# A four-layer graph network with a mixture of experts: the gates applied in the expert loop, the mean taken from the stored rows, no meeting ahead of the output pass

## The reference

```python
m = segment_sum(h[src], dst) * rsqrt(deg_in)
x = m @ W_gc + b_gc + feats @ W_res + b_res
vals, idx = top_k(x @ Wg + bg, 2)
gates = softmax(vals)                       # two gates a node
h1 = gelu(rows_of_expert @ w1[e] + b1[e])
y_s = h1 @ w2[e] + b2[e]                    # one row for each (node, pick)
core = zeros(N, D).at[tok_s].add(g_s[:, None] * y_s)
y = x + core
mean, var = mean(y, axis=0), mean((y - mean) ** 2, axis=0)
out = (y - mean) * rsqrt(var + 1e-5) * gamma + beta
# and around it: x = layernorm(x + out)
```

## Time and profile before

| | us |
|---|---|
| median of three runs | 2047.52 |
| lowest and highest | 2045.85, 2050.57 |
| span of the profiled execution | 2045.9 |
| TensorE busy in it | 1805.1 (88%) |
| VectorE, ScalarE, GpSimd busy | 887.9, 498.7, 492.5 |
| expert loop, from the first chunk of steady work to the last rows | about 1615 to 1935 |
| from the last expert rows to the output pass | 1935 to 2011 |
| output pass | 2011 to 2046 |

### The profile page before, as it was taken

One profiled execution on the slowest core, in us unless ns is written; L12 is line 12 of the kernel. 1 busy time (PEld: TensorE's weight loads), 2 busy tenths in 40 slices (PEclk: granted clock), 3 DMA queues, 4 the chain that ended last, 5 costly groups with the idle time before them and its releaser, 6 DMA issues. The chain is left out here.

```text
span 2045.9 us, 34276 instructions
## 1 busy us (share of the span) xinstructions
PE 1805.1 (88%) x9529; PEld 1440.3 (70%) x9563; DVE 887.9 (43%) x2701; ACT 498.7 (24%) x1301; POOL 492.5 (24%) x858
## 2 busy tenths in 40 slices
PE   4888885999899989999999999989999699999830
PEld 2455554788688868878878878867777588888720
DVE  7877663444534421122321137756766212222145
ACT  0134444322222311111111111111111132232252
POOL 1021222311111100000000002216666632332244
PEclk7999997999999989999999999989999799999955
DMA  4188999999678858877768888868876699999931
GB/s 129 53 293 299 318 317 354 311 327 319 224 259 269 263 182 290 291 243 241 239 213 289 289 266 290 290 212 260 258 250 199 209 377 374 375 375 375 351 127 63
DMA packets 279214, 545.09 MB, mean 266 GB/s; under 512 B 18214, under 2 KB 201040, under 8 KB 275920
## 3 DMA queue, kind: packets, MB, share of 16 engines
q1 hardware_dynamic: 269280, 525.30, 77.1%
q0 software_dynamic: 8032, 17.60, 2.3%
q10 hardware_dynamic: 1808, 1.08, 0.3%
HBM read 415.19 MB, written 128.72 MB: 266 GB/s over the span
## 5 line engine op out<-in xcount | busy, mean ns | idle before, releaser
L1069 PE MATMUL psum<-xsa,blk 128*128 128x512 f32 x2500 | 642.2, 406 | 17.8 <-DVEq L381 8.2
L1069 PEld LDWEIGHTS psum<-xsa,blk 128*128 128x128 f32 x2500 | 462.9, 191 | 106.9 <-issue 11.1
L1069 PE MATMUL psum<-xsb,blk 128*128 128x512 f32 (+1 forms) x1875 | 415.7, 369 | 5.9 <-DVEq L381 5.9
L1069 PEld LDWEIGHTS psum<-xsb,blk 128*128 128x128 f32 x1875 | 321.8, 190 | 64.6 <-issue 7.2
L1835 POOL TENSOR_SCALAR ve<-mv 128x1 f32<-128x1 f32 x75 | 16.9, 225 | 802.6 <-DVE mv L1546 802.6
L1431 DVE TENSOR_SCALAR onehots<-counts_scratch 128x348 bf16<-128x348 f16 x464 | 161.7, 373 | 87.8 <-issue 47.1
L971 PE MATMUL psum<-onehots 128*128 128x349 bf16 x464 | 149.4, 322 | 40.3 <-DVE onehots L1436 38.2
L563 PE MATMUL psum<-route,expert_weights 128*128 128x128 f32 x1360 | 170.9, 280 | 0.1
L974 PE MATMUL psum<-zrow 128*128 128x512 bf16 x431 | 164.8, 390 | 0.0
L563 PEld LDWEIGHTS psum<-route,expert_weights 128*128 128x128 f32 x1360 | 161.4, 195 | 1.3 <-DVE route L675 0.5
L573 PE MATMUL psum<-expert_weights,route 128*128 128x256 f32 x672 | 159.1, 380 | 0.0
(11 more groups left out here) (309 smaller groups left out, 2077.4 us busy)
## 6 DMA issues: line engine op xcount, KB each, us to landing
blk<-counts_src_on_rows SPq DMA_DIRECT2D x125, 832.0 KB, 5.2
blk<-counts_src_on_rows SPq DMA_DIRECT2D x125, 768.0 KB, 4.8
expert_weights<-in_L_gnn_w SPq DMA_DIRECT2D x176, 512.0 KB, 6.0
blk<-counts_dst_on_rows SPq DMA_DIRECT2D x50, 832.0 KB, 4.5
counts_dst_on_rows<-band_rows SPq DMA_DIRECT2D x25, 1600.0 KB, 8.2
blk<-counts_dst_on_rows SPq DMA_DIRECT2D x50, 768.0 KB, 4.2
counts_src_on_rows<-blk SPq DMA_DIRECT2D x13, 1600.0 KB, 8.7
counts_src_on_rows<-rblk SPq DMA_DIRECT2D x12, 1600.0 KB, 9.8
```

What stands on the lines that cost most here:

```text
L1069: mm = e.matmul(o, blk[n][:, k * P:(k + 1) * P], XS[:, k, :, 0:Fw], start=(k == 0), stop=(k == T - 1 and not own))
```

## The change

Each pick's gate travels with its number. In the last graph pass ScalarE takes one Exp a tile (`gap_exp`, behind `picks_made`) and GpSimd makes the two gates by three one-column operations at the head of its turn (`l3_gates`). `ids` has two columns, pick number and gate; unused rows have gate 0. SP loads both columns, TensorE turns both, and VectorE keeps `pick_of` and `gate_of`. In the expert loop VectorE scales b2 by the gate and makes `yout` = product * gate + scaled b2. It then adds `yout` to V2, so that after the loop V2 + R2 is the sum of y over each partition; R2 is the sum of X4 over the tiles, made ahead of the loop. One product with ones gives the mean, and X4 is centred before the stored rows are back. The stored rows lie now by partition (`ybuf` row p * 50 + 2t + k), and no engine scales them. GpSimd adds nothing any more: TensorE adds all 25 tiles of squares. The `combine` meeting is gone, and several one-time semaphores are joined (`bn_steps`, `ident_set`).

```diff
+            def l3_gates(i, par):
+                e.wait_ge(S("gap_exped"), i + 1)
+                if i:
+                    e.wait_ge(S("gates_made"), 3 * i)
+                e.tensor_scalar(exps[:, 1:2], exps[:, 0:1], 1.0, None, ALU.add).then_inc(S("gates_made"), 1)
+                e.wait_ge(S("gates_made"), 3 * i + 1)
+                e.tensor_tensor(pick[:, i, 0, 1:2], exps[:, 1:2], minus[:, :], ALU.pow).then_inc(S("gates_made"), 1)
+                e.wait_ge(S("gates_made"), 3 * i + 2)
+                e.tensor_tensor(pick[:, i, 1, 1:2], exps[:, 0:1], pick[:, i, 0, 1:2], ALU.mult).then_inc(S("gates_made"), 1)
             def l3_ids(i, par):
+                e.wait_ge(S("gates_made"), 3 * (i + 1))
                 for k in range(TOP):
                     e.indirect_dma_start(out=ids, out_offset=bass.IndirectOffsetOnAxis(ap=slot_to[:, k, i:i + 1], axis=0),
-                                         in_=pick_id[:, k, i:i + 1], in_offset=None).then_inc(S("ids_scattered"), 16)
+                                         in_=pick[:, i, k, :], in_offset=None).then_inc(S("ids_scattered"), 16)
...
-            pipeline(e, [(2, l3_first), (1, l3_keep), (2, l3_scatter), (2, l3_last), (2, l3_ids)], unrolled=True)
+            pipeline(e, [(2, l3_gates), (2, l3_first), (1, l3_keep), (2, l3_scatter), (2, l3_last), (2, l3_ids)], unrolled=True)
...
+            def gap_exp(i, par):
+                e.wait_ge(S("picks_made"), i + 1)
+                if i:
+                    e.wait_ge(S("gates_made"), 3 * i)
+                e.activation(exps[:, 0:1], top_val[:, i, 0:1], ACT.Exp, scale=-1.0, bias=top_val[:, i, 1:2])\
+                    .then_inc(S("gap_exped"), 1)
+            run("l3", [low("l3", F, ndst), (2, gap_exp), (1, copy("l3", "x_turned", "xT", flat(tT2), pT2)),
...
-            e.dma_start(pick_rows[0:NCH, :], ids[0:NCH * P, :].rearrange("(c p) a -> c (p a)", p=P)).then_inc(S("inputs_loaded"), 16)
+            e.dma_start(pick_rows[0:NCH, :, :], ids[0:NCH * P, :].rearrange("(c p) a -> c p a", p=P)).then_inc(S("inputs_loaded"), 16)
...
-                e.dma_start(picked_rows[:, lo:hi, :, :].rearrange("p t k f -> p t (k f)"),
-                            ybuf[TOP * lo * P:TOP * hi * P, :].rearrange("(t p k) f -> p t (k f)", t=hi - lo, p=P))\
+                e.dma_start(picked_rows[:, lo:hi, :, :].rearrange("p t k f -> p (t k f)"),
+                            ybuf[0:TOP * NP, :].rearrange("(p r) f -> p (r f)", p=P)[:, TOP * lo * F:TOP * hi * F])\
                     .then_inc(S(f"outs_in{g}"), 16)
...
-            phase_end(e, "combine")
...
+            for a in range(2):
+                mm = e.transpose(psum[:, 6, a * NCH:(a + 1) * NCH], pick_rows[0:NCH, :, a], identF[0:NCH, 0:NCH])
+            mm.then_inc(S("ids_turned"), 1)
...
+            e.wait_ge(S("node_sums"), 1)
+            e.matmul(psum[:, 0, 0:F], ones[:, :], V2[:, :], start=True, stop=True).then_inc(S("bn_summed"), 1)
+            for g, (lo, hi) in enumerate(COMBINED):
+                e.wait_ge(S("squared"), g + 1)
+                for t in range(lo, hi):
+                    mm = e.matmul(psum[:, 1, 0:F], ones[:, :], picked_rows[:, t, 1, :], start=(t == 0), stop=(t == T - 1))
+            mm.then_inc(S("bn_summed"), 1)
...
-                        e.activation(v, v, ACT.Copy, scale=gate[:, k, t:t + 1]).then_inc(S("picks_scaled"), 1)
...
+            e.wait_ge(S("tile_x4_kept"), past("l3", "x4_kept") + T)
+            st.done(e.tensor_reduce(R2[:, :], X4[:, 0:T - 1, :].rearrange("p t f -> p f t"), AX.X, ALU.add))
+            st.done(e.scalar_tensor_tensor(R2[:, :], X4[:, T - 1, :], valid[:, T - 1:T], R2[:, :], ALU.mult, ALU.add))
+            e.memset(V2[:, :], 0.0).then_inc(S("rows_added"), 1)
             e.wait_ge(S("ids_turned"), 1)
+            e.tensor_copy(pick_of, psum[:, 6, 0:NCH]).then_inc(S("picks_known"), 1)
+            st.done(e.tensor_copy(gate_of, psum[:, 6, NCH:2 * NCH]))
...
+                    e.wait_ge(S(f"b2_in{n}"), 16 * j + 16)
+                    carry_wait(e)
+                    e.tensor_scalar(b2s[n], b2s[n], gate_of[:, bass.ds(c, 1)], None, ALU.mult).then_inc(S("bias_scaled"), 1)
+                    e.wait_ge(S("bias_scaled"), c + 1)
                     e.wait_ge(S("chunk_summed"), c + 1)
-                    e.wait_ge(S(f"b2_in{n}"), 16 * j + 16)
                     e.wait_ge(S(f"rows_stored{n}"), 16 * j)
-                    e.tensor_tensor(yout[n], psum[:, 4 + par, 0:F], b2s[n], ALU.add)\
+                    carry_wait(e)
+                    e.scalar_tensor_tensor(yout[n], psum[:, 4 + par, 0:F], gate_of[:, bass.ds(c, 1)], b2s[n], ALU.mult, ALU.add)\
                         .then_inc(S("chunk_made"), 1)
+                    e.wait_ge(S("rows_added"), c + 1)
+                    e.wait_ge(S("chunk_made"), c + 3)
+                    carry_wait(e)
+                    e.tensor_tensor(V2[:, :], V2[:, :], yout[n], ALU.add).then_inc(S("rows_added"), 1)
...
+            e.tensor_tensor(V2[:, :], V2[:, :], R2[:, :], ALU.add).then_inc(S("node_sums"), 1)
+            e.wait_ge(S("bn_summed"), 1)
+            st.done(e.tensor_scalar(G[:, :], psum[:, 0, 0:F], 1.0 / N, None, ALU.mult))
+            for g, (lo, hi) in enumerate(COMBINED):
+                e.tensor_tensor(X4[:, lo:hi, :], X4[:, lo:hi, :], G[:, :].unsqueeze(1).to_broadcast([P, hi - lo, F]), ALU.subtract)\
+                    .then_inc(S("centred"), 1)
+            e.wait_ge(S("centred"), len(COMBINED))
+            for g, (lo, hi) in enumerate(COMBINED):
+                e.wait_ge(S(f"outs_in{g}"), 16)
...
-                        ins = e.tensor_tensor(added[:, n, :], added[:, n, :], v, ALU.add)
...
-            phase_end(e, "combine")
```

107 lines of the change are left out of this document (29 added, 78 removed).

## The result

The changed kernel takes 2025.8 us (median of four runs, 2024.4 to 2034.3) against 2048.2 us of the kernel before in the same session (2045.9 to 2050.6). The ratio is 0.990 with an interval of 0.9886 to 0.9914. That is a gain of 22 us where 35 were forecast, and the time lies above the range of 2008.5 to 2021. The profiled execution has a span of 2023.2 us, 22.7 less than before.

The account below looks back on a forecast made before the run. TensorE was taken to bound the expert loop, three waits the tail. 2045.9 - 30.6 - 4.9 + 0.05 + 0.6 + 0.25 = 2011.3 us of span, plus 1.6 to the median, rounded to 2013; range 2008.5 to 2021.

Parts of the forecast that it names:

- What bounds the kernel: Whole kernel: TensorE busy 99.87 of 100 us in the loop; behind it gate products, GpSimd's additions and the meeting.
- Parts 1 and 2: Tail and meeting, behind the expert loop: variance read 30.6 us sooner, and 4.9 us less without the meeting.
- The covered centring: Tail: VectorE's added work and centring, 10.1 us plus hand-overs, hidden behind the stored rows' way out and back.
- the rise of the clock: Tail: TensorE's denser squares bring its clock to full during the second or third group.
- The meeting's 4.9: Ahead of the output pass: without the all-engine meeting, 0.05 us remains of 4.98, 4.9 us less.
- Rival (a): Tail: TensorE stays at the low clock, squares end at 1978.0 in place of 1971.0, time 2020; chance 0.11.
- Part 3: Expert loop: VectorE's added work is hidden, 0 taken, bounds 0 and 4.9 us; plus 0.05 at the loop's end.
- Part 4: Ahead of the loop: 0.6 us delay from the sum of X4 and 0.25 for the second transpose of picks.
- 1.3 us of small operations: Ahead of the loop: VectorE's work between the sum of X4 and the third chunk's copy.
- rival (b): Added work shows: 1 KB step twice as dear, third chunk 10 us late, 2022; with other bounds 2015 to 2024; chance 0.15.
- Part 5: Last graph pass: later Exp and GpSimd's gate operations fit in idle time; 0 taken, bounds 0 and 2.5 us.
- a tile of the graph pass longer than before: Graph pass: one of the signs listed as showing the forecast wrong.

Follow-up runs that it names:

- repeated: Second profile of each kernel, the kernel before and the changed one, unchanged, in another session on one chip: 2050.0 and 2028.1 us.
- e9_one_small_buffer: Changed kernel with exps and minus in one small buffer, putting the node rows back at byte 125056: 2014.0 us, ratio to before 0.9829.
- e10: Changed kernel with exps and minus in one buffer and the sum of X4 taken tile by tile inside the last graph pass: 2008.7 us.
- e1: Changed kernel without the sum of X4 ahead of the loop (R2 stays 0): 2024.1 us.
- e8_before_moved_32: Kernel before with an unused buffer of 32 bytes ahead of the node rows, which puts them at byte 125088: 2061.1 us against 2047.9.

## Why the prediction missed

**What bounds the kernel** held: loop, tail and chain were as read the earlier trace rows.

**Parts 1 and 2**, -35.5 us forecast, -38.1 measured. The covered centring and the rise of the clock came as told. Counted from the last expert rows, VectorE was to begin the last group at 27.8 us and did so at 26.1 (1975.19), since the stored rows came in faster than the 395 GB/s that I took from the earlier trace rows: 433 GB/s in the first row of the windows above. The third group began 18.7 us behind the last rows (before 19.8), and six tiles then took 3.68 us each time, VectorE's own pace, not the loads' forecast 4.0. From the last group's start to the variance 8.9 us were forecast and 8.3 measured (TensorE's last six tiles took 2.86 us, not 3.4). The term that was mis-sized is the rate of the loads, by 1.8 us of gain. The DMA share was 1.02 at 433 GB/s and 1.08 at 375 in the earlier trace rows, so a full share doesn't mean one rate. The meeting's 4.9 was right to 0.1. Rival (a), the low clock throughout, fell: only the first group's products and most of the second's ran at it.

**Part 3**, the loop at nothing: 15 profiles of kernels with the gates in the loop have 319.7 to 324.8 us, on average 321.4, the three with the old loop 319.1 to 320.8, on average 319.9. So some 1.5 us, inside the bound of 4.9. The two ranges overlap, so this is near the scatter, and neither the row sum nor the product-and-sum accounts for it by itself. TensorE is still busy 99.91 of 100 us, as in the earlier trace rows:

```profile
1700.00:1800.00 100.00, 99.91 (x680) 89.09 (x679) 39.74 (x104) 29.73 (x104) 30.20 (x51) 1.00 1.07 372
```

**Part 4**, +0.85: measured +1.3 in the changed kernel (+1.7 repeated): 2.5 for the sum, less about 1 that I put down to an earlier load of the picks (last section). The size of the reduction was right; the mis-sized term is what comes behind it, the small correction that ended with GpSimd's additions (2.64 us). From the reduction to the third chunk's copy it took 4.3 us, where the prediction had "1.3 us of small operations". I had charged GpSimd's presence to the reduction, which stayed under the forecast made without it. 1 KB steps twice as dear, the condition of rival (b), did not occur: its late third chunk has the cause in the correction, not in the step.

**Part 5**, 0 with a bound of 2.5: +0.9.

**The step that failed** is one that the prediction has no line for. It took every stretch that the diff does not touch as unchanged, and the sum as the span plus the touched parts. Four such phases gave 13.8 us away. The prediction named the sign for it, "a tile of the graph pass longer than before", and thought of added waits. The full diff has the new buffers, and the order of allocation says what moves; that a move of 32 bytes costs time was shown by no row at hand before the result. With that step mended by `e9_one_small_buffer`, the span is 2012.3 us (forecast 2011.3) and the median 2014.0 (forecast 2013). That this is so near is in part luck: the tail gained 4 us more than forecast, and small terms that were put at nothing or too low took about as much.

| term | forecast | measured (e9, before repeated) |
|---|---|---|
| tail and meeting | -35.5 | -39.5 |
| loop | 0 | +1.5 (all profiles) |
| ahead of the loop | +0.85 | +1.5 |
| last graph pass | 0 | +0.9 |
| output pass | 0 | +0.7 |
| h1a, h1b, h2a, h2b at the old place | 0 | +0.2 |
| the same at the new place | 0 | +13.8 |

So the right forecast of the mechanism and the wrong total go together: rival (b), whose 2015 to 2024 lies nearest, was right in kind only for 4 to 5 us of small terms, and these were paid by the tail. The 2022 that it had for a late third chunk lies near the measured 2025.8 by chance.

## What to carry to other kernels

Diff the addresses too. A new small buffer can move everything that is allocated behind it, and phases that the change does not touch can become 3% slower. Take the stretches of the old and the new profile side by side, from start to end, before explaining a total. And where TensorE streams one buffer against another without a pause, try the distance between the two as a parameter: an unused buffer of 32 bytes costs nothing to test, and here it cost 13 us in 2048.

## What the hardware showed

- In h1a, h2a and h2b the spacing of back-to-back products of 512 columns depends on the distance between the streamed operand and the blocks: 226.7 ns at distance 0 modulo 1024, 228.9 at 64, 232.4 (sometimes 233.3) at 128, 233.3 at 32. Nothing waits in the records, and the clock is 1.00 in all. That the blocks are the other party is what the runs leave over, as said above. The Trainium skill, SBUF — State Buffer, section "Who interferes with whom", gives TensorE two independent read ports, one for the moving operand and one for the weight load, and says that it never waits on anyone. By that rule the distance could not matter. The measurement decides, and here it does.
- VectorE beside GpSimd: a reduction with one operand took 10.83 us, no more for each number (1.76 ns) than the one of the earlier trace rows (1.84), but an operation on two operands (2.64 us where 0.48 is usual) and a scaling (4.94 us in `e10`, 5.21 in `e1`, where 0.34 is usual) ended when GpSimd's additions did. The same section of the Trainium skill says that a reduction never contends and that an operation with two inputs in SBUF contends with a GpSimd operation that reads SBUF; both agree with these rows, and the scaling is of a kind that it lists as able to take the shared ports.
- A strided read of one number per KB costs 10.83 us for 6144, 1.76 ns each, against 1.15 for contiguous ones; the earlier trace rows had it at 1.84. The Trainium skill, VectorE: DVE Perf Modes, section "Mode 1× (REGULAR) — the baseline", names no further cost for odd strides; these rows disagree. No run separates the stride from the kind of instruction: the contiguous rows are an addition, the strided ones sums over 24 or 25 numbers.
- The last scatter of pick numbers landed sooner in the kernels that scatter 8 bytes a row than in those with 4. From its issue to the load that waits for it: 7.7 us before (7.8 repeated, 7.3 in `e8_before_moved_32`), 3.6 us after (3.6 repeated, 3.5 in `e9_one_small_buffer`). I take the 1 us of part 4 to come from here; no run shows it. Nor does any isolate the width from the changed layout of the table. The rows are the kernel before, repeated, and then `e9_one_small_buffer`:

```profile
1598.39 0.96 POOL L1866 DMA_INDIRECT pick_of_row<-pick_id,slot_to  x1 [0.31 <-issue]
1606.16 0.33 SPq L498 DMA_DIRECT2D route<-pick_of_row  x1
```
```profile
1598.38 0.96 POOL L1868 DMA_INDIRECT pick_and_gate_of_row<-pick,slot_to  x1 [0.30 <-DVEq L651]
1601.88 0.33 SPq L494 DMA_DIRECT2D route<-pick_and_gate_of_row  x1
```
